# Local attention layers: the band mask is added by VectorE between PSUM and SBUF, no longer by a TensorE matmul

## What is computed

```python
# 8 heads of 64, window 64, each of the two layers over x of 8 x 512 x 128
bq = q.reshape(b, h, w, WINDOW, d) * QK_SCALE
bk, bv = look_around(k), look_around(v)        # a window and the one before it: 128 keys
sim = jnp.einsum('bhwid,bhwjd->bhwij', bq, bk)
mask = (i < j) | (i > j + WINDOW) | (j == -1)
sim = jnp.where(mask, -jnp.finfo(sim.dtype).max, sim)
attn = jax.nn.softmax(sim, axis=-1)
out = jnp.einsum('bhwij,bhwjd->bhwid', attn, bv)
```

## Times and profile before

| | |
|---|---|
| Median of 3 runs | 2360.86 us (2351.46 to 2368.8) |
| The profiled execution | 2359.08 us, its span 2357.3 us |
| Local layers, first to last row maximum (L2325) | 1580.2 to 2299.2 us of the span |
| Slices in them | 64 |
| Band matmuls (L1993) | 128, 38.6 us of busy time |
| Row maxima (L2325) | 64, mean 1224 ns |
| Exponentials (L2157) | 512, mean 466 ns |

### The profile page before, as it was taken

The page is one execution under the profiler, slowest core; times in us unless marked ns, Lnnn a source line. Parts: engine busy times, 40 slices in busy tenths (PEclk is TensorE's granted clock), DMA queues, the critical chain, the costliest instruction groups (busy, mean ns, idle before and its releaser), DMA issues. The chain is left out here.

```text
span 2357.3 us, 41683 instructions
## 1 busy us (share of the span) xinstructions
PE 1867.0 (79%) x12868; PEld 958.0 (41%) x12868; DVE 1410.5 (60%) x2466; ACT 1162.7 (49%) x2814; POOL 929.6 (39%) x1035
## 2 busy tenths in 40 slices
PE   4589999866358338898878987748999999999996
PEld 2244444425246222333323321425555555555552
DVE  3466666633311326676556664347888888888882
ACT  1155555540023003665456656016767776777672
POOL 3144455431320421222112210136666666766660
PEclk9599999885579556998889889569999999999996
DMA  3233333322123321332332231221111111111110
GB/s 102 63 124 121 118 127 114 124 76 82 39 76 99 107 87 63 106 109 81 108 108 102 98 106 64 68 88 36 36 38 29 45 38 36 54 39 37 39 52 20
DMA packets 137889, 180.17 MB, mean 76 GB/s; under 512 B 14896, under 2 KB 82355, under 8 KB 137520
## 3 DMA queue, kind: packets, MB, share of 16 engines
q1 hardware_dynamic: 135728, 174.59, 23.5%
q0 software_dynamic: 2048, 4.16, 0.7%
HBM read 97.22 MB, written 66.06 MB: 69 GB/s over the span
## 5 line engine op out<-in xcount | busy, mean ns | idle before, releaser
L1169 DVE TENSOR_REDUCE M_sb<-banks 128x1 f32<-128x512 f32 (+3 forms) x1024 | 551.3, 583 | 377.4 <-PE banks L775 214.3
L968 ACT ACTIVATE probs_sb<-banks 128x512 f32<-128x512 f32 (+3 forms) x1024 | 479.3, 516 | 387.9 <-PE banks L812 386.1
L775 PE MATMUL banks<-K_sb,Q_sb 72*128 72x512 bf16 (+3 forms) x1024 | 384.9, 381 | 135.6 <-DMA V_sb<-v_dram 122.1
L812 PE MATMUL banks<-Q_sb,K_sb 75*128 75x512 bf16 (+3 forms) x1024 | 368.2, 366 | 10.4 <-ACT probs_sb L968 5.2
L775 PEld LDWEIGHTS banks<-K_sb,Q_sb 72*128 72x128 bf16 x1024 | 106.8, 104 | 412.8 <-DVE M_sb L1169 164.3
L826 PE MATMUL banks<-probs_sb,V_sb 128*32 128x512 f32 (+3 forms) x2048 | 255.9, 569 | 8.6 <-POOL probs_sb L1059 3.5
L2157 ACT ACTIVATE l_p_sb<-banks,l_nb_sb,l_inv_sb 128x128 f32<-128x128 f32 x512 | 228.1, 466 | 12.9 <-DVE l_nb_sb L2329 12.7
L2243 POOL TENSOR_TENSOR l_pn_sb<-l_p_sb,l_rs_sb 128x512 f32<-128x512 f32 x128 | 150.2, 1173 | 149.6 <-DVE l_rs_sb L2335 148.1
L2235 POOL TENSOR_TENSOR l_inv_sb<-l_clip_sb,l_minus_half_sb 128x16 f32<-128x16 f32 x64 | 186.2, 2910 | 57.1 <-DVE l_clip_sb L2304 55.2
L2228 POOL TENSOR_TENSOR l_ts_sb<-l_t_sb 128x1024 f32<-128x1024 f32 x64 | 153.3, 2396 | 40.9 <-DVE l_t_sb L2283 24.0
L812 PEld LDWEIGHTS banks<-Q_sb,K_sb 75*128 75x128 bf16 x1024 | 104.5, 103 | 115.9 <-issue 29.9
(11 more groups left out here) (244 smaller groups left out, 3482.2 us busy)
## 6 DMA issues: line engine op xcount, KB each, us to landing
Q_sb<-qk_dram SPq DMA_DIRECT2D x192, 96.0 KB
v_dram<-vpad_sb SPq DMA_DIRECT2D x16, 1024.0 KB, 5.6
V_sb<-v_dram SPq DMA_DIRECT2D x64, 256.0 KB
o_dram<-osum_sb SPq DMA_DIRECT2D x64, 256.0 KB, 4.6
l_vs_sb<-l_vt_sb SPq DMA_DIRECT2D x112, 128.0 KB, 2.3
qk_dram<-parts_sb SPq DMA_DIRECT2D x96, 128.0 KB
K_sb<-qk_dram SPq DMA_DIRECT2D x32, 288.0 KB
x_norm_sb<-x SPq DMA_DIRECT2D x24, 256.0 KB, 2.7
```

The lines of the kernel that those rows point to most:

```text
L775: mm = pe.matmul(out[:, 0:width], g.Q[0:RK, slot, h, k * P:(k + 1) * P], g.K[0:RK, slot, hk(h), 0:width], start=True, stop=not causal)
L812: pe.matmul(SB[ring % 3][:, t0:N], g.K[0:RM, q, hk(h), k * P:(k + 1) * P], g.Q[0:RM, q, h, t0:N], start=True, stop=True).then_inc(s["b_sco ...
L968: act.activation(g.probs[:, k, h, t0:N], SB[ring % 3][:, t0:N], ACT.Exp, scale=scale)\
L1169: dve.reduce_max(g.M[:, u % 2, k, h:h + 1], SA[ring % 3][:, 0:width], AX.X, negate=True)\
```

## The change

`scores` no longer adds the mask: the two band matmuls go, a matmul with one column (its result is overwritten by the first score) stands in their place, and the score matmuls write (`start=True`) and do not add. DVE's `maxima` gets an instruction ahead of the maximum: it adds `bandf`, broadcast over the 8 heads, to the 1024 columns of `SB` and writes the masked scores to a new SBUF tile, `l_sc`, with two buffers (slices take turns). The maximum and ACT's exponentials read this tile. PE's `scores` of the next slice waits for that addition (semaphore `masked`), and no longer for the exponentials. The addition itself also waits for the exponentials of two slices before, which read the same buffer. The bf16 copy of the mask, and the cast that makes it, are gone.

```diff
--- before.py
+++ after.py
@@ -1712,7 +1712,6 @@
     g.turn = g.sb("l_turn", [P, 2, 2, 2, CH, HD])
     g.minus_half = g.sb("l_minus_half", [P, 2, 2 * PAIRS])
     g.bandf = g.sb("bandf", [P, 2, P])
-    g.band = g.sb("band", [P, 2, PAIRS, P], BF16)
 
     g.xs = g.sb("l_xs", [P, N])
     g.lsq = g.sb("l_sq", [P, 2, 2 * PAIRS, HD])
@@ -1728,6 +1727,7 @@
     g.kr = g.sb("l_kr", [P, PAIRS, W + N])
     g.vt = g.sb("l_vt", [P, CH, INNER])
     g.vs = g.sb("l_vs", [P, CH, INNER])
+    g.lsc = g.sb("l_sc", [P, 2, 2, PAIRS, P])
     g.lmx = g.sb("l_mx", [P, 2, 2, PAIRS])
     g.lnb = g.sb("l_nb", [P, 2, 2, PAIRS])
     g.lsm = g.sb("l_sm", [P, 2, 2, PAIRS])
@@ -1757,7 +1757,7 @@
         "setup", "xr_loaded", "xf_loaded", "proj", "sq", "ss", "clip", "inv", "t1", "t2", "tsum", "kn",
         "qk_turned", "qk", "v_psum", "v", "scores", "max", "nbias", "exp", "rsum", "pnorm",
         "turned", "pt", "pv", "o", "wo", "x1", "s2", "mean", "xc", "sq2", "var", "veps", "rstd", "spread", "rstd_psum",
-        "xh", "h", "gate_psum", "gate", "gelu", "value_psum", "hidden", "y2", "x2", "final", "stored")}
+        "masked", "xh", "h", "gate_psum", "gate", "gelu", "value_psum", "hidden", "y2", "x2", "final", "stored")}
     g.v_shifted = [g.sem(f"l_v_shifted{c}") for c in range(CH)]
     g.xs_loaded = [g.sem(f"l_xs_loaded{c}") for c in range(CH)]
     s = g.ls
@@ -1776,7 +1776,6 @@
             dve.memset(g.minus_half[:, :, :], -0.5)
             dve.memset(g.graw[:, :, :], 0.0)
             dve.wait_ge(s["setup"], 8 * 16)
-            dve.tensor_copy(g.band[:, :, :, :], g.bandf[:, :, :].unsqueeze(2).broadcast_to([P, 2, PAIRS, P]))
             for layer in range(2):
                 for w in range(2):
                     dve.tensor_tensor(
@@ -1988,10 +1987,9 @@
             def scores(it, t):
 
                 pe.wait_ge(s["qk"], it * 2 * CH + 2 * t + 2)
-                pe.wait_ge(s["exp"], it * 2 * CH + 2 * t)
-                for e in range(2):
-                    pe.matmul(SB[:, e, :], g.identb[:, :], g.band[:, min(t, 1), :, :].rearrange("p h n -> p (h n)"),
-                              start=True, stop=False, skip_group_check=True)
+                pe.wait_ge(s["masked"], it * CH + t)
+                pe.matmul(SB[:, 0, 0:1], g.identb[:, :], g.identb[:, 0:1], start=True, stop=True,
+                          skip_group_check=True)
                 for p in range(PAIRS):
                     for j in range(2):
                         at = t * P + j * W
@@ -1999,7 +1997,7 @@
                             mm = pe.matmul(SB[W * j:W * (j + 1), e, p * P:(p + 1) * P],
                                            g.qr[HD * e:HD * (e + 1), p, at:at + W],
                                            g.kr[HD * e:HD * (e + 1), p, at:at + P],
-                                           start=False, stop=True, skip_group_check=True)
+                                           start=True, stop=True, skip_group_check=True)
                 mm.then_inc(s["scores"], 1)
 
             def turn(it, t, e):
@@ -2154,7 +2152,7 @@
                 act.wait_ge(s["pnorm"], after(it, 2 * CH, 2 * t + e - 3))
                 for p in range(PAIRS):
                     head = 2 * p + e
-                    last = act.activation(g.pe_[:, t % 2, e, p, :], SB[:, e, p * P:(p + 1) * P], ACT.Exp,
+                    last = act.activation(g.pe_[:, t % 2, e, p, :], g.lsc[:, t % 2, e, p, :], ACT.Exp,
                                           bias=g.lnb[:, t % 2, e, p:p + 1], scale=g.linv[:, t, 0, head:head + 1],
                                           accum_out=g.lsm[:, t % 2, e, p:p + 1])
                 last.then_inc(s["exp"], 1)
@@ -2322,7 +2320,13 @@
             def maxima(it, t):
                 at = it * CH + t
                 dve.wait_ge(s["scores"], at + 1)
-                dve.tensor_reduce(g.lmx[:, t % 2, :, :], SB[:, :, :].rearrange("p e (h n) -> p e h n", h=PAIRS),
+                dve.wait_ge(s["exp"], after(it, 2 * CH, 2 * t - 2))
+                dve.tensor_tensor(g.lsc[:, t % 2, :, :, :].rearrange("p e h n -> p (e h) n"),
+                                  SB[:, :, :].rearrange("p e (h n) -> p (e h) n", h=PAIRS),
+                                  g.bandf[:, min(t, 1), :].unsqueeze(1).broadcast_to([P, NH, P]), ALU.add)\
+                   .then_inc(s["masked"], 1)
+                dve.wait_ge(s["masked"], at + 1)
+                dve.tensor_reduce(g.lmx[:, t % 2, :, :], g.lsc[:, t % 2, :, :, :],
                                   AX.X, ALU.max, negate=True).then_inc(s["max"], 1)
                 dve.wait_ge(s["max"], at + 1)
                 dve.wait_ge(s["inv"], at + 1)
```

## The result

The changed kernel takes 2441.9 us in the median of 4 runs (2430.73 to 2442.7), the kernel before 2364.83 us in 4 runs (2351.46 to 2372.93). The ratio is 1.0327 with a 95% interval of 1.0294 to 1.036: 77 us slower. The direction was forecast, the size was not: 47 us were forecast, and 2441.9 lies above the range's end of 2432.

What follows compares the result with a forecast made beforehand. Bound taken as a loop alternating between TensorE and VectorE in the local layers. First iteration 3.5 us, 15 others x 2.95 = 44.3, less 0.69 for the cast: +47, giving 2408 us, range 2390 to 2432.

Steps and rivals of the forecast that it cites:

- The loop: Local layers, TensorE and VectorE alternating through scores, maximum and rotation: iteration 2.95 us longer, 49.1 instead of 46.1.
- my sum: Delays followed through one iteration's slices: +0.88, +1.78, +2.66 behind slices 1, 2, 3, then +2.95 in all; chance 0.77.
- Saving on TensorE: Band matmuls ahead of the scores replaced by one 1-column matmul: 0.35 us saved a slice, bounds 0.31 and 0.43.
- VectorE's pass: Addition between scores and bias: 1.25 us, less 0.02 for the maximum reading SBUF, +1.23 a slice, bounds 1.19 and 1.30.
- Slice 3 and 0: TensorE sets slice 3's start, +2.66 behind it; in slice 0 VectorE is at +1.92, ahead of the scores at +2.31.
- the stall that the prediction saw in L2304: Small VectorE instruction seeming to wait for GpSimd's: addition possibly 0.3 us late, 15 x 0.3 = +5, left as an option.
- The clock: Rival: clock falls because TensorE idles more, to 0.97; its 542 us grow by 16, giving 2424; chance 0.05.
- a granted clock under 0.97 in the stage: Sign listed as showing the forecast wrong; the clock was expected at 1.00 in the local layers.
- The hidden pass: Rival: VectorE's addition is hidden, TensorE sets the pace and only its saving remains: 2338 us; chance 0.02.
- the two slices that TensorE leads: Rival: TensorE sets the pace in slices 2 and 3, each -0.35; about 0.4 us an iteration, 2367; chance 0.06.
- ScalarE as the pace for its source: Rival: ScalarE becomes the pace, the 12 us added to exponentials reading SBUF lie on the path: 2420; chance 0.05.
- VectorE as the bound everywhere: Rival: VectorE bounds every slice, no gain from TensorE's shorter part, 64 x 1.23 = 79 us, 2439; chance 0.05.

Runs made afterwards that it cites:

- e2: Kernel before without the two band matmuls (one 1-column matmul instead), nothing added on VectorE, mask left out: 2337.0 us, ratio 0.9891.
- e4: Changed kernel with ScalarE's exponentials reading the unmasked scores from PSUM, as in the kernel before: 2437.2 us, ratio 1.0333.
- e3: Changed kernel with the two band matmuls put back, so the mask is added twice: 2457.3 us, ratio 1.0426.
- e7: Kernel before with the mask addition as an extra, unread VectorE pass in slice 1 alone: 2411.5 us, ratio 1.0211.
- e8: Kernel before with the mask addition as an extra, unread VectorE pass in slice 3 alone: 2395.7 us, ratio 1.0118.
- e5: Changed kernel with unused filler matmuls on TensorE during its waits, 8 in slice 1 and first-iteration slices, 2 in slice 0: 2408.0 us, ratio 1.0178.
- e1: Changed kernel with unused filler matmuls on TensorE, 16 in slice 1 and first-iteration slices, 4 in slice 0: 2432.1 us, ratio 1.0298.
- e11: Changed kernel with TensorE turning the older slice's first half after the scores, and ScalarE squaring the projection before copying turned halves: 2418.1 us, ratio 1.021.

## Why the forecast missed, step by step

- **The loop, right in size, in part by luck.** The steady iteration was forecast at 49.1 and is 49.16 where the clock holds. The intervals between the additions of slices 1, 2, 3, 0 and 1 were 10.89, 11.79, 11.95 and 14.46 by my sum; in the iteration from 2158.98 they are 10.91, 11.83, 12.02 and 14.40.
- **Saving on TensorE, 0.35 forecast.** It is 0.43, my upper bound. The one-column matmul keeps the scores off for 0.10 us, from L1991's start at 2168.54 to L1997's at 2168.63, where the band took 0.53; and e2 gave 0.42 a slice.
- **VectorE's pass, 1.23 forecast.** From start to start the addition takes 1.26 us (2158.98 to 2160.24) and the maximum is no shorter for reading SBUF, so 1.26.
- **Slice 3 and 0, wrong in the mechanism.** "Its wait of 0.74 for ACT ahead of the second reciprocal is used up, so DVE is at +1.92": that takes ScalarE's exponentials of slice 3 as not moved. The chain in order of time (start us, us, engine, line) shows that they move, since the table load itself stands behind the wait for the bias.

```profile
2184.23 0.18 DVE l_nb_sb L2333
...
2184.49 1.28 ACT L2155
...
2185.79 0.06 ACT l_p_sb L2155
...
2190.72 0.05 DVE l_rs_sb L2339
...
2193.74 1.22 DVE l_sc_sb L2324
```

The load (1.28 us, ACT L2155) starts at 2184.49, after the bias. In the kernel before, the load of that slice began at 2165.26, at once behind a copy, the bias being there already. Now VectorE still waits for the exponentials, 0.49 us ahead of the reciprocal at 2190.72: from slice 1's start to this reciprocal it takes 31.74 us, against 28.91 before (2171.19 - 2142.28), so +2.83. My sum has 1.92 + 0.35 = 2.27 for that distance, since it lets slice 1 start 0.35 earlier. VectorE then comes late to slice 0: the addition has no idle time before it.

Yet e4 shows that the exponentials don't set this start. There they end earlier, the reciprocal comes 31.45 us after slice 1's start at 2252.63, and the addition of slice 0 comes after 34.76 us, as in the changed kernel (2193.74 - 2158.98). What stands between is the small L2302 (L2303 in e4), and it ends with GpSimd's instruction in both. The changed kernel, and e4:

```profile
2192.08 1.05 POOL L2241 TENSOR_TENSOR l_pn_sb<-l_p_sb,l_rs_sb 128x512 f32<-128x512 f32 x1
...
2192.55 0.61 DVE L2302 TENSOR_SCALAR l_clip_sb<-l_ss_sb 128x16 f32<-128x16 f32 x1
```

```profile
2285.74 1.04 POOL L2242 TENSOR_TENSOR l_pn_sb<-l_p_sb,l_rs_sb 128x512 f32<-128x512 f32 x1
...
2285.90 0.91 DVE L2303 TENSOR_SCALAR l_clip_sb<-l_ss_sb 128x16 f32<-128x16 f32 x1
```

It starts 0.3 us earlier in e4, takes 0.3 longer, and ends 0.03 after GpSimd's again. This is the stall that the prediction saw in L2304 and left out of its sum ("one term may go either way"). Redone with the measured saving of 0.43 and pass of 1.26, the sum gives +0.83, +1.76 and +2.59 behind slices 1, 2 and 3, and 2.16 + 1.26 - 0.59 = 2.83 for the iteration; the other 0.2 of the measured 3.02 are VectorE's late start in slice 0. So a saving taken too small stood for a stall left out, and that 2.95 is so near to 3.02 is luck.
- **The clock, the step that failed.** I gave a lower clock a chance of 0.05 and a price of 16 us, and the sum takes TensorE's longer waits to cost it nothing but their length. The prediction had named the sign, a granted clock under 0.97 in the stage: it is 0.96 in the 14 iterations. The lower clock was there in 13 of 14 iterations, in the first iteration (0.82 against 0.91) and in the last two slices (0.79 against 1.00). It costs 19 to 22 us in the 14 iterations, and part of what the two ends add: 3.8 us beyond the loop in the first iteration, and 5.7 us in the last two slices, of which a part is the loop's. Together with 40 to 46 us of the loop this makes the stage 75.6 us longer, and the medians 77 apart. I had worked out TensorE's share after the change, 86%, and it was right. The row for 87% had 0.97, and I took that for harmless. In the same trace two iterations with a dip took 47.26 and 47.60 instead of 46.14: a dip costs 1.1 to 1.5 us, and one in each of 16 iterations makes 18 to 23 us, 2426 to 2431 in all. That belonged in the likeliest case, though it would still have been 11 to 16 us short. My price of 16 was too low as well, but the larger error is the chance.
- **Rivals.** The hidden pass (2338) and the two slices that TensorE leads (2367) are out by e3 (4.59 us an iteration for the four passes) and by e7 and e8, where one pass costs 1.15 in slice 1 and 0.96 in slice 3. ScalarE as the pace for its source is out by e4. VectorE as the bound everywhere, 2439, gives nearly the measured time by a wrong mechanism: its iteration would be 4 x 1.23 longer, 51.1, without any lower clock, and e5 shows 49.17.

## To carry to other kernels

When an edit moves work from TensorE to another engine on one loop with it, price the wait twice: its length on the loop, and what the granted clock does behind it. Look for the few iterations of the trace before in which the clock already fell, take their extra time as the price of one dip, and ask in how many iterations the edit makes the same wait longer. A filler on TensorE shows whether the clock is the cause, if it is sized to end before the wait does: e1's was too long and told little, e5's was half as long and told it.

## What the hardware showed that was not expected

- The same wait of 2.39 us on TensorE is followed by matmuls at the full rate in one iteration and at half of it in another: 0.60 and 1.06 us for four transposes. Longer iterations can bring more dips though the wait in slice 1 is unchanged (e8: 7 of 14, every second one, at 47.1 us; before: 2 of 14 at 46.14). What sets this is open.
- A longer loop can be outweighed by a steadier clock: e11's clean iteration is 0.46 us longer than the changed kernel's, and its 14 iterations are 15 us shorter.
- A small VectorE instruction (L2302, 128x16, SBUF to SBUF) that starts while GpSimd runs one of its own ends with it. Of the 64 in the changed kernel's trace, 34 start so, and each ends 0.03 or 0.04 us after GpSimd's instruction, however long that takes; the other 30 take 0.17 or 0.18. That the one waits for the other is read from these ends and from e4; no run changed GpSimd's work alone.
- A scalar exponential that also sums comes every 480 ns from SBUF and every 438 from PSUM. Their own rows, 483 and 467, hide most of that, as they overlap with their neighbours'.
- A reduction over 1024 columns of the masked scores takes 1220 ns from SBUF, and 1224 from PSUM.
